# First block's input projection: 2 KB weight rows, four open accumulations, and no wait of TensorE for its own products

## What is computed

```python
x = x + gnn(layernorm(x), ...)            # 10 propagation steps over 21250 edges
x = x + lstm(layernorm(x)[None], ...)[0]

def lstm_step(carry, x_t):                # S = 4 sets of weights, 4 gates of 512
    h, c = carry
    logits = concat([h, c, x_t]) @ W_sel.T + b_sel
    onehot = one_hot(argmax(logits), S)
    g_all = einsum('bi,sgi->bsg', x_t, W_ih) + einsum('bh,sgh->bsg', h, W_hh) + b_ih + b_hh
    g = einsum('bsg,bs->bg', g_all, onehot)
    h2, c2 = lstm_activate(g, c)          # sigmoid and tanh of the four gates
    return (h2, c2), h2
```

## Time and profile before

| | |
|---|---|
| median of 3 runs | 6861.82 us |
| profiled execution, its own time | 6865.91 us |
| span of its profile | 6864.2 us |
| PE busy | 6126.8 us (89%) |
| PEld busy | 4106.7 us (60%) |
| DVE busy | 3617.9 us (53%) |
| ACT busy | 1804.5 us (26%) |
| POOL busy | 1685.8 us (25%) |
| the projection's matmuls (L983) | 512 pairs, from 1274.0 to 1436.1 us of the span |
| TensorE's clock in that stretch | 0.50 of full speed |

### The profile page before, as it was taken

One profiled execution on the slowest core, in us unless ns is written; L12 is line 12 of the kernel. 1 busy time (PEld: TensorE's weight loads), 2 busy tenths in 40 slices (PEclk: granted clock), 3 DMA queues, 4 the chain that ended last, 5 costly groups with the idle time before them and its releaser, 6 DMA issues.

```text
span 6864.2 us, 340774 instructions
## 1 busy us (share of the span) xinstructions
PE 6126.8 (89%) x126674; PEld 4106.7 (60%) x126675; DVE 3617.9 (53%) x19152; ACT 1804.5 (26%) x6561; POOL 1685.8 (25%) x4128
## 2 busy tenths in 40 slices
PE   6727999679999999999999999999999999999986
PEld 3423444566666666666666666666666666666664
DVE  5453111235555556555665555566556665565555
ACT  1001000412233233222332332233333333233321
POOL 5732111412222222222222222222222222222220
PEclk8758999579999999999999999999999999999999
DMA  3220000522222122222222222222222222222210
GB/s 94 1 77 0 0 0 0 177 70 60 60 61 61 57 61 62 58 60 61 64 63 61 62 61 61 60 62 64 61 61 63 64 63 61 60 63 61 61 52 27
DMA packets 715589, 389.97 MB, mean 57 GB/s; under 512 B 47835, under 2 KB 703579, under 8 KB 715296
## 3 DMA queue, kind: packets, MB, share of 16 engines
q1 hardware_dynamic: 684322, 369.66, 18.4%
q0 software_dynamic: 24192, 0.10, 1.1%
q10 hardware_dynamic: 7038, 19.69, 0.9%
HBM read 370.96 MB, written 18.38 MB: 57 GB/s over the span
## 4 chain that ended last, share of the span: by engine, by line
PE 70%; issue 6%; DVE 6%; DMA 0%; DVEq 0%; SPq 0%; POOL 0%; ACT 0%; POOLq 0%
PE ps L1007 33%; PE ps L1069 15%; PE ps L1016 8%; PE ps L1000 5%; PE ps L996 4%; DVE hsum L837 2%; PE ps L993 2%; PE ps L983 2%; DVE osum L845 1%; DVE acts L855 1%; DVE gates L842 1%; DVE osum L848 1%; DVE cprod L851 0%; PE ps L972 0%; DMA wring<-in_w_ih 0%
## 5 line engine op out<-in xcount | busy, mean ns | idle before, releaser
L1007 PE MATMUL ps<-WH,hparts 128*2 128x384 f16 x49760 | 2297.3, 326 | 194.4 <-issue 173.2
L837 DVE TRANSPOSE_TENSOR_REDUCE hsum<-ps 128x12 f32<-128x384 f32 x1250 | 728.8, 583 | 1784.5 <-PE ps L1007 1774.2
L1007 PEld LDWEIGHTS ps<-WH,hparts 128*2 128x2 f16 x49760 | 1042.4, 83 | 1046.7 <-issue 297.0
L1069 PE MATMUL ps<-xcur,wcur 128*128 128x64 f32 x9728 | 1342.8, 281 | 89.1 <-issue 15.1
L1069 PEld LDWEIGHTS ps<-xcur,wcur 128*128 128x128 f32 x9728 | 1179.3, 191 | 276.6 <-issue 213.6
L449 POOL COPY xT<-hfull 128x4 f32 x1250 | 239.5, 192 | 3721.7 <-DVE hfull L866 3721.7
L465 POOL COPY wcur<-wring 128x512 f32<-128x512 f32 x1216 | 743.4, 611 | 449.7 <-ACT gxb L593 447.8
L1016 PEld LDWEIGHTS ps<-WH,hparts 128*2 128x2 f16 x40000 | 596.7, 83 | 359.0 <-issue 316.6
L1016 PE MATMUL ps<-WH,hparts 128*2 128x128 f16 x40000 | 775.4, 219 | 8.6
L578 ACT ACTIVATE gx_now<-gxb 128x16 f32 x1250 | 269.7, 216 | 1832.6 <-DVE pick L831 1709.3
L963 PE MATMUL ps<-O,Adj 128*128 128x512 f16 x3000 | 650.3, 380 | 77.2 <-DVEq L743 77.2
(11 more groups left out here) (147 smaller groups left out, 5001.8 us busy)
## 6 DMA issues: line engine op xcount, KB each, us to landing
wring<-in_w_ih SPq DMA_DIRECT2D x1280, 256.0 KB, 2.9
gxb<-in_w_hh ACTq DMA_DIRECT2D x32, 512.0 KB, 4.0
adjacency<-Adj SPq DMA_DIRECT2D x2, 6400.5 KB, 24.7
Adj<-adjacency SPq DMA_DIRECT2D x10, 640.0 KB, 7.3
sim<-adjacency SPq DMA_DIRECT2D x10, 640.0 KB, 6.5
adjacency<-total,where_ POOLq DMA_INDIRECT x168
x_rows<-X SPq DMA_DIRECT2D x1, 2560.0 KB, 8.7
wring<-x_rows SPq DMA_DIRECT2D x10, 256.0 KB, 3.6
```

Source lines behind the costliest of these rows:

```text
L837: dve.tensor_reduce(hsum[:, :], gate_ps.rearrange("p (c q) -> p c q", q=32), AX.X, ALU.add, apply_transpose=True).then_inc(turned, 1)
L1007: last = nc.tensor.matmul(gate_ps[32 * j:32 * j + 2, :], hparts[:, k, :], WH[:, s * KC + k, part, j, 0:3 * P], start=(k == 0 and part == 0 ...
L1069: last = nc.tensor.matmul(unit_ps, wcur[:, k, :], xcur[:, k, :], start=(k == 0), stop=(k == KC - 1))
```

## The change

SP's ring now holds for each slot one quarter of the inputs for all four units of a round. The transfer reads one run of 2 KB for each partition (128 runs instead of 512, the same 256 KB). PE goes through a round by k first and by unit inside, so that four accumulations are open at once, one in each of the banks 4 to 7. The unit's product is announced (`proj_mm`) by its last matmul at k = 3. A slot is given back by the last matmul of its pass itself (`wring_free` for k = 0 to 2); for k = 3 SP waits for the round's four `proj_mm` instead. The wait of PE for its own product and the two separate increments of `wring_free` and their waits go. DVE's credits are 3 for `wring_free` and 4 for `proj_mm`, and its waits for `proj_mm` move up by 4. The number of matmuls, of transfers and of bytes is the same, as are the operands' shapes. The loads of later blocks keep the old layout.

```diff
@@ sync @@
             with sp.Fori(0, S) as q:
                 for g in range(G):
-                    for u in range(SUB):
-                        sp.wait_ge(wring_free, sp.snap(q * (G * SUB) + (g * SUB + u + 1)))
-                        load_unit(q, g, u)
+                    for k in range(KC):
+                        if k < KC - 1:
+                            sp.wait_ge(wring_free, sp.snap(q * (G * (KC - 1)) + (g * (KC - 1) + k + 1)))
+                        else:
+                            sp.wait_ge(proj_mm, sp.snap(q * (G * SUB) + (g * SUB + SUB)))
+                        sp.dma_start(wring[:, k, :, :].rearrange("p u n -> p (u n)"),
+                                     w_ih[:, bass.ds(q, 1), order[g], k * D:(k + 1) * D].rearrange("p a n -> p (a n)")
+                                     ).then_inc(wring_in[k], 16)
...
-            sp.wait_ge(wring_free, UNITS + SUB)
+            sp.wait_ge(proj_mm, UNITS + SUB)
@@ vector @@
             dve.sem_inc(proj_out, SUB)
-            dve.sem_inc(wring_free, SUB)
+            dve.sem_inc(wring_free, KC - 1)
+            dve.sem_inc(proj_mm, SUB)
...
-                    dve.wait_ge(proj_mm, dve.snap(q * SUB + (u + 1)))
+                    dve.wait_ge(proj_mm, dve.snap(q * SUB + (SUB + u + 1)))
...
-            dve.wait_ge(proj_mm, UNITS)
+            dve.wait_ge(proj_mm, UNITS + SUB)
@@ tensor @@
             with pe.Fori(0, SG) as q:
-                for u in range(SUB):
-                    pe.wait_ge(wring_in[u], pe.snap(q * 16 + 16))
-                    pe.sem_inc(pieces_seen, 1)
-                    pe.wait_ge(proj_out, pe.snap(q * SUB + (u + 1)))
-                    for k in range(KC):
-                        last = nc.tensor.matmul(ps[:, 4 + u, 0:TB], wring[:, u, k, :], xT[:, k, 0:TB], start=(k == 0), stop=(k == KC - 1))
-                    last.then_inc(proj_mm, 1)
-                    pe.wait_ge(proj_mm, pe.snap(q * SUB + (u + 1)))
-                    pe.sem_inc(wring_free, 1)
+                for k in range(KC):
+                    for u in range(SUB):
+                        if u == 0:
+                            pe.wait_ge(wring_in[k], pe.snap(q * 16 + 16))
+                            pe.sem_inc(pieces_seen, 1)
+                        if k == 0:
+                            pe.wait_ge(proj_out, pe.snap(q * SUB + (u + 1)))
+                        last = nc.tensor.matmul(ps[:, 4 + u, 0:TB], wring[:, k, u, :], xT[:, k, 0:TB], start=(k == 0), stop=(k == KC - 1))
+                        if k == KC - 1:
+                            last.then_inc(proj_mm, 1)
+                        elif u == SUB - 1:
+                            last.then_inc(wring_free, 1)
```

## The result

The changed kernel took 6817.65 us (median of 4 runs, 6817.24 to 6818.73) against 6863.39 us of the kernel before beside it: a ratio of 0.9933 (95% interval 0.9917 to 0.9949), 45.7 us faster. The forecast was 6814 us, in a range of 6784 to 6838. The profiled execution took 6817.24 us with a span of 6815.5 us.

The account below looks back on a forecast made before the run. PE's waits for its own products bound the projection. 109.3 us of pairs + 3 + 1.5 + 1 = 114.8 us instead of 162.1, with 0.7 at the start 48 us gained: 6814 us, range 6784 to 6838.

Parts of the forecast that it names:

- What bounds, and that the gain arrives: Projection stage of 162 us: PE's waits for its own products bound it, and its gain goes straight to the end.
- POOL's slack: POOL's wait before its first step work, 95.0 us in the kernel before; a sign expected at about 47 us.
- The pace of 0.213 us: Projection's unbroken load-and-matmul pairs: 0.213 us each, set by the operand's load; 512 pairs and the last end take 109.3 us.
- (a) The ring, 3 us: Refilling ring slots: hidden after W_hh, 0.1 us late beside it; 3 us taken, bounds zero and 12.7 us.
- (b) The rows: Ring loads: 2 KB rows make room for the pace beside W_hh, 383 against 282 GB/s at full share.
- (c) and (d), bank and turn: DVE freeing banks: 1.5 us taken, bounds 0 and 4.5; the loop's turn: 1 us in all, bounds 0 and 7.8.
- (f) The start: Ring's first piece, queued on SP behind the guesses' single-word store; later pieces come 0 to 1.5 us earlier, 0.7 taken.
- The clock: TensorE's clock in the projection stage: stays at 0.50 (1.2 GHz), as unbroken work alone does not raise it.
- the first rival: Projection at full clock (2.4 GHz): the ring binds, 71 us gained, 6791 us; chance 7%.
- the forecast's remark on the ring: At full clock in the projection, waits for the ring would break the run again, which speaks against that clock.
- 48 gaps of 0.43 us: Gaps between the projection's units, 20.6 us, beside 15 of 0.95 us and a further 1.6 us of a transfer's.
- The rival on the steps: The 1250 steps: moved code slows branches; at 0.06 us a step 27 us slower, 6889; slower 4%, smaller loss 4%.

Follow-up runs that it names:

- e5: The changed kernel with ACT beginning W_hh only behind the projection, so the ring is alone on the DMA engines, slower by design; 6909.24 us, one run.
- e6: The changed kernel with 128 moving columns instead of 64 in the projection's matmuls; 6799.61 us, ratio 0.9909 to the kernel before.
- e1: The kernel before without PE's wait for its own product, SP waiting for proj_mm instead; unit order and 512-byte runs stay; 6813.10 us, ratio 0.9936.
- e2: The changed kernel with PE's wait for its own product put back, once for each pass; 6838.92 us, ratio 0.9972 to the kernel before.
- e8: e4 with the guesses turned by a PE transpose first, so their store is 10 rows of 512 bytes; 6805.68 us, ratio 0.9912 to the kernel before.
- e4: The changed kernel with the guesses' single-word store moved from SP, ahead of the ring, to ACT behind W_hh; 6815.96 us, ratio 0.9937 to the kernel before.
- e10: The kernel before, own waits kept, with 128 moving columns instead of 64 in its projection; 6818.50 us, ratio 0.9945 to the kernel before.
- e3: e1 with W_ih laid out so that a unit's load is one 2 KB run per partition, old order kept; 6812.95 us, ratio 0.9934 to the kernel before.

## Why the prediction was right, and where it was not

**What bounds, and that the gain arrives.** Right. The stage gained 44.8 us and the time 45.7. POOL's slack of 50.3 us (47 forecast) and the unchanged rest (5425 and 5435 us in two traces of the changed program, 5428 before) show it.

**The pace of 0.213 us.** Right, and the term that carried the sum: 0.2134 in e5, 0.2135 in the longest run of the changed kernel. That the operand's load sets it, which I took from L972 with 4 columns, is shown by e6 before its clock rises: the same pace with 128.

**(a) The ring, 3 us.** The mechanism was right, the size a little low. Beside W_hh the landing was 5.0 us, not 4.3, as the ring asked for more (in e1, with the old rows at the same pace, it was 4.9); 7 waits of 3.0 us came of it. But PE's busy time is 112.9 us too, against 109.5 in e5: each break also leaves the end of a last product uncovered (0.2 us), which for 9 breaks is some 2 us; the rest is not placed. 117.3 - 109.5 = 7.8 us (6.5 in the second trace) is what the ring and banks cost in all, against 3 + 1.5 + 1 in the sum. All of it is W_hh's neighbourhood, as e5 shows.

**(b) The rows.** Wrong, without harm to the sum. I let a store of 2 KB rows at 383 GB/s stand for such a load, and concluded that these rows make the room for the pace beside W_hh. By share the loads with 2 KB reach 278 to 292 GB/s behind W_hh, against 279 to 289 with 512 bytes, and e1 had nearly the whole gain with the short runs. The sum held in spite of this, since its term (a) was taken from the landings of the old, 512-byte form. The Trainium skill (DMA: Bandwidth & Descriptors, Specifications) gives 512 B as the least transfer for line rate. I had said that the trace disagrees with it; the loads agree with it behind W_hh. Beside W_hh, at the unbroken pace, the longer runs bring 7 to 9% by share (315 against 338 and 343 GB/s) and 2.3 to 3.6 us of the stage, and nothing in the times; at the slower pace of the kernel before and e2 it is 320 against 324.

**(c) and (d), bank and turn.** 1.2 us of waits for DVE and nothing at the turn, against 1.5 and 1 taken. In e5 both are zero.

**(f) The start.** 0.7 us sooner was forecast; 1.0 later came in the first trace and 1.5 sooner in the second, so the runs can't tell. That the single-word store holds the first piece was right: turning the guesses (e8) brings it 7 to 9 us sooner. That it is only a place in SP's queue was wrong, by e4: on ACT's queue it stalls the ring as well.

**The clock.** Right for 64 columns: it stays at 0.50 through 109.48 us of unbroken work, so the first rival is refuted for this form. The Trainium skill (TensorE: Matmul & The Clock Gate, Part 1) says that sustained activity releases the throttle; read simply, that does not hold for this stream. Whether the work is unbroken did not decide the rise: with 96 or 128 columns the clock rose, in e10 between gaps of 0.43 us. In one thing the forecast's remark on the ring was right, since beside W_hh each of those kernels lost the clock again for some us behind waits for the ring; yet waits of 1.97 to 2.12 us in e6 (from 1295 to 1324 us) were followed by no fall. What decides it is not shown. I had the right rows for a no, and did not ask what would make it a yes, which is worth more than the change's rows and order.

**A count.** The forecast has 48 gaps of 0.43 us and 1.6 us besides; the waits show 47 (20.6 us), and the 48th is the transfer's 1.6 us. Nothing in the sum hangs on it.

**The rival on the steps.** Nothing of it is seen: 5425 and 5435 us in the same program scatter more than any difference to 5428. That code in another place can never cost was not tested.

**What the change is made of.** Its own title names three parts. The wait is the whole of it (e1), the open accumulations bring nothing by themselves (e3), and the rows bring 2.3 to 3.6 us of the stage beside W_hh, by four traces.

## What to carry to other kernels

An engine that waits for its own product in order to hand back a buffer pays twice, here with a gap of 0.43 us and with 0.2 us of overlap between the last product and the next; let the last instruction carry the increment and whoever refills the buffer wait for it. Take the pace of an unbroken run from another line of the same trace that loads the same operand, not from a group that contains the gaps. When an operand's load sets the pace and the clock is at its lower level, try wider products before anything else: here 128 columns cost no time at 0.50 of full clock, and with 96 the clock rose where with 64 it did not.

## What the runs showed of the hardware that I had not expected

- Pairs of an fp32 128 x 128 load and a matmul of 64 columns, unbroken for 109.48 us, left TensorE's clock at 0.50 of full (1.2 GHz); the same loads with 96 and 128 columns went to 1.00 (2.4 GHz), with 128 from 0.213 to 0.136 us a pair.
- In the kernel before with 128 columns (e10) the clock rose between gaps of 0.43 to 1.02 us. It fell twice behind waits of 1.78 and 2.20 us, and from 1326 us on it stayed up between gaps of 0.43 to 0.95 us.
- A store of 5 KB in 1280 single words takes 11.8 us from its issue to its landing in e4, on ACT's queue, and meanwhile PE stands for 6.4 us until a piece of SP's queue lands. As 10 rows of 512 bytes (e8) it was followed by no wait.
- Behind a wait for an own product the gap was 0.43 us where a wait for `proj_out` followed, and 0.30 us in e2 where it didn't; that this wait makes the difference is argued above.
